# Sorting x by a permutation kept in fp32, in place of three bf16 parts of x

## The reference

```python
mask = (adj > 0.0).astype(x.dtype)
W1a, W1b = (W1[:F], W1[F:])
xj_proj = x @ W1a
diff = x[:, :, None, :] - x[:, None, :, :]
h = jax.nn.relu(xj_proj[:, :, None, :] + diff @ W1b + b1)
hm = jnp.einsum('bjkh,bjk->bjh', h, mask)
deg = jnp.sum(mask, axis=-1)
out = hm @ W2 + deg[..., None] * b2
x = _layernorm(x + out, axis=-1)
```

## Time and profile before

| | us |
|---|---|
| median of 3 runs (307.5 to 307.82) | 307.55 |
| the profiled execution | 308.28 |
| its span, first to last instruction | 306.2 |
| PE busy | 278.8 (91%) |
| DVE busy | 272.8 (89%) |
| ACT busy | 239.5 (78%) |
| POOL busy | 99.2 (32%) |

### The profile page before, as it was taken

The page is one execution under the profiler, slowest core; times in us unless marked ns, Lnnn a source line. Parts: engine busy times, 40 slices in busy tenths (PEclk is TensorE's granted clock), DMA queues, the critical chain, the costliest instruction groups (busy, mean ns, idle before and its releaser), DMA issues. The chain is left out here.

```text
span 306.2 us, 9122 instructions
## 1 busy us (share of the span) xinstructions
PE 278.8 (91%) x2601; PEld 209.3 (68%) x2601; DVE 272.8 (89%) x987; ACT 239.5 (78%) x706; POOL 99.2 (32%) x166
## 2 busy tenths in 40 slices
PE   0496999999999999999999999999999999999960
PEld 0253676877777877868787777777786877776750
DVE  2886699999999999999999999999999999989761
ACT  2338788889898989899898989898979889876500
POOL 1306142313334342434232343433342323304111
PEclk9999899999999999999999999999999999999985
DMA  7920303030211303030402112030304020100000
GB/s 205 371 99 1 89 0 105 3 98 9 57 66 28 96 19 106 14 108 0 120 0 79 40 35 85 17 103 17 103 1 120 0 56 2 35 3 18 19 17 21
DMA packets 28833, 18.12 MB, mean 59 GB/s; under 512 B 17537, under 2 KB 28033, under 8 KB 28802
## 3 DMA queue, kind: packets, MB, share of 16 engines
q1 hardware_dynamic: 28802, 17.76, 19.7%
HBM read 15.65 MB, written 2.10 MB: 58 GB/s over the span
## 5 line engine op out<-in xcount | busy, mean ns | idle before, releaser
L1024 PE MATMUL ring<-hot,vh 128*128 128x256 bf16 (+3 forms) x448 | 96.7, 268 | 1.0 <-ACT ring L740 1.0
L1024 PE MATMUL ring<-hot,vl 128*128 128x256 bf16 (+3 forms) x448 | 96.2, 267 | 0.0
L740 ACT COPY ring<-um 128x512 f32<-128x512 f32 (+2 forms) x144 | 65.9, 474 | 19.5 <-DVE small L1302 10.8
L1293 DVE SCALAR_TENSOR_TENSOR sm<-ring,sm 128x512 f32<-128x512 f32 (+2 forms) x144 | 73.0, 507 | 7.0 <-PE ring L1024 3.3
L1293 DVE SCALAR_TENSOR_TENSOR st<-ring,st 128x256 f32<-128x256 f32 (+2 forms) x144 | 48.0, 334 | 5.5 <-PE ring L1030 2.1
L1024 PEld LDWEIGHTS ring<-hot,vh 128*128 128x128 f16 x448 | 43.9, 98 | 11.9 <-issue 7.3
L1269 DVE TENSOR_SCALAR hot<-slotT 128x1024 bf16<-128x1024 f16 (+2 forms) x144 | 49.2, 373 | 0.0
L740 ACT COPY ring<-ut 128x512 f32<-128x512 f32 (+7 forms) x128 | 38.5, 338 | 13.0 <-DVE st L1293 11.0
L1024 PEld LDWEIGHTS ring<-hot,vl 128*128 128x128 f16 x448 | 44.1, 98 | 2.6
L1030 PE MATMUL ring<-hot,vh 128*64 128x512 bf16 (+3 forms) x256 | 44.7, 353 | 0.0
L533 POOL TENSOR_TENSOR vl<-vf,vh 128x384 f16<-128x384 f32 x32 | 28.6, 914 | 47.0 <-ACT vh L702 47.0
(11 more groups left out here) (106 smaller groups left out, 560.6 us busy)
## 6 DMA issues: line engine op xcount, KB each, us to landing
adj_sb<-adj SPq DMA_DIRECT2D x16, 512.0 KB, 4.1
x_sb<-x SPq DMA_DIRECT2D x16, 128.0 KB, 2.2
x_all<-x SPq DMA_DIRECT2D x4, 512.0 KB, 7.9
xT_sb<-xT SPq DMA_DIRECT2D x16, 128.0 KB, 3.8
out<-o_sb SPq DMA_DIRECT2D x16, 128.0 KB, 2.0
wts<-weights SPq DMA_DIRECT2D x1, 513.0 KB, 4.8
cst_general<-general SPq DMA_DIRECT2D x1, 256.0 KB, 6.3
cst_half<-half SPq DMA_DIRECT2D x1, 113.5 KB, 3.5
```

The lines of the kernel that those rows point to most:

```text
L740: eng.copy(view(segment, ring[unit % BANKS]), u).then_inc(seeded, 1)
L1024: last = eng.matmul(b[:, g * n:g * n + n], part[side][:, g * NT + k, 0:P], selection(g * NT + k), start=(s == 0 and not seeds), stop=(s == ...
L1293: eng.scalar_tensor_tensor(out=to, in0=v, scalar=0.0, in1=to, op0=ALU.max, op1=ALU.add).then_inc(added[tile], 1)
```

## The change

`perm` is made in fp32. The upper 16 bits of an fp32 one or zero are a bf16 one or zero, so the three readers that need bf16 read every second bf16 number (`perm16`). `sort_x` multiplies x by `perm` once, both in fp32. The four functions that split x, their tiles and their semaphores are gone. Since `sort_x` now reads `x_sb` itself, the load of x two pairs later waits for it too.

```diff
-        perm = both("perm", [P, TILES, P], BF16)
+        perm = both("perm", [P, TILES, P])
...
+        def perm16(side, c):
+
+            return perm[side][:, c, :].bitcast(BF16).rearrange("p (r two) -> p r two", two=2)[:, :, 1]
+
...
                 if not pair.general and pair.follows(2):
                     eng.wait_ge(xb_ready, pair.n - 1)
+                    eng.wait_ge(xs_ready, pair.n - 1)
                 eng.dma_start(x_sb[pair.side][:, :, :], x_v[pair.data]).then_inc(x_loaded[pair.side], 16)
...
-            def rest_x(pair):
...
-                eng.tensor_tensor(xr[:, :, :], x_sb[pair.side][:, :, :], xh[:, :, :],
-                                  ALU.subtract).then_inc(xr_ready, 1)
-
-            def low_x(pair):
...
-                eng.tensor_tensor(xl[:, :, :], xr[:, :, :], xm[:, :, :], ALU.subtract).then_inc(xl_ready, 1)
...
             def residual(pair):
                 eng.wait_ge(db_ready, pair.n + 1)
+                eng.wait_ge(x_loaded[pair.side], 16 * (pair.half + 1))
...
-                if has(2):
-                    low_x(second)
...
-                    rest_x(third)
                     neg_keys(third)
                     degree_bias(third)
...
-                eng.copy(xh[:, :, :], x_sb[pair.side][:, :, :]).then_inc(xh_ready, 1)
...
-                eng.copy(xm[:, :, :], xr[:, :, :]).then_inc(xm_ready, 1)
...
                 if has(2):
-                    high_x(second)
                     copy_degrees(second)
...
                 if has(2):
-                    middle_x(second)
                     ranks(second)
...
                           last = eng.matmul((bx1, bx2)[g][:, at:at + P], mask[pair.side][:, g * NT + t, k * P:k * P + P],
-                                          perm[pair.side][:, g * NT + t, :], start=True, stop=True)
+                                          perm16(pair.side, g * NT + t), start=True, stop=True)
...
             def sort_x(pair):
-                eng.wait_ge(xl_ready, pair.n + 1)
+                eng.wait_ge(x_loaded[pair.side], 16 * (pair.half + 1))
                 eng.wait_ge(perm_ready, pair.n + 1)
                 eng.wait_ge(maskT_copied, 2 * pair.n + 2)
-                parts = (xh, xm, xl)
                 for t in range(NT):
-                    for s, part in enumerate(parts):
-                        for g in range(2):
-                            last = eng.matmul(bx2[g * F:g * F + F, t * P:t * P + P], part[:, g * NT + t, :],
-                                              perm[pair.side][:, g * NT + t, :], start=(s == 0),
-                                              stop=(s == len(parts) - 1), skip_group_check=True)
+                    for g in range(2):
+                        last = eng.matmul(bx2[g * F:g * F + F, t * P:t * P + P], x_sb[pair.side][:, g * NT + t, :],
+                                          perm[pair.side][:, g * NT + t, :], start=True, stop=True,
+                                          skip_group_check=True)
                 last.then_inc(xs_ready, 1)
...
-                    last = eng.transpose(to[:, c * P:c * P + P], perm[pair.side][:, c, :], ident[:, :])
+                    last = eng.transpose(to[:, c * P:c * P + P], perm16(pair.side, c), ident[:, :])
```

More of the change, by code:

```diff
@@ L299, in build @@
         db = both("db", [P, TILES, F])
[L301 to L304, removed]
         xs = sb("xs", [P, N])
@@ L358, in build @@
         db_ready, xb_ready = sem("db_ready"), sem("xb_ready")
-        xh_ready, xr_ready = sem("xh_ready"), sem("xr_ready")
-        xm_ready, xl_ready = sem("xm_ready"), sem("xl_ready")
         xs_ready, xs_copied = sem("xs_ready"), sem("xs_copied")
@@ L586, in _ @@
             eng.wait_ge(consts_loaded["single"], 16)
-            rest_x(Pair(0, 0))
             neg_keys(Pair(0, 0))
             degree_bias(Pair(0, 0))
-            low_x(Pair(0, 0))
-            rest_x(Pair(0, 1))
             neg_keys(Pair(0, 1))
             degree_bias(Pair(0, 1))
-            low_x(Pair(0, 1))
             low_v(Pair(0, 0), 0)
@@ L598, in _ @@
             residual(Pair(0, 0))
-            rest_x(Pair(0, 2))
             neg_keys(Pair(0, 2))
@@ L608, in general @@
                 degree_bias(pair)
-                rest_x(pair)
-                low_x(pair)
                 low_v(pair, 0)
@@ L809, in _ @@
             eng.wait_ge(consts_loaded["single"], 16)
-            high_x(Pair(0, 0))
             copy_degrees(Pair(0, 0))
-            middle_x(Pair(0, 0))
             ranks(Pair(0, 0))
@@ L819, in _ @@
             look_over(Pair(0, 0))
-            high_x(Pair(0, 1))
             copy_degrees(Pair(0, 1))
@@ L823, in _ @@
             copy_u_tail(Pair(0, 0))
-            middle_x(Pair(0, 1))
             ranks(Pair(0, 1))
@@ L834, in general @@
                 copy_degrees(pair)
-                high_x(pair)
                 ranks(pair)
-                middle_x(pair)
                 for g in range(2):
@@ L914, in excesses @@
                     last = eng.matmul(bx3[:, c * P:c * P + P], deg16[pair.side][:, c:c + 1].to_broadcast([P, P]),
-                                      perm[pair.side][:, c, :], start=pair.general,
+                                      perm16(pair.side, c), start=pair.general,
                                       stop=(pair.general or c == TILES - 1), skip_group_check=True)
```

## The result

| | before | changed |
|---|---|---|
| median on the same chip, us | 307.69 | 310.43 |
| the profiled execution, us | 308.28 | 310.44 |
| its span, us | 306.2 | 308.4 |

The ratio is 1.0085 [1.0067, 1.0103]: slower by 0.9%, as forecast in sign; the time is 1.1 us above the 309.3 that I gave. A disturbed execution of the changed kernel (334.98 us) counts in the median of the table and not in the ratio; the other three have a median of 310.41.

What follows compares the result with a forecast made beforehand. PE was taken as the bound, with DVE close behind at 97%. Terms 1.7 + 0.3 + 0.1 - 0.3 gave +1.8 us: 310.1 for the profiled execution, 309.3 for the median, range 307.7 to 316.5.

Steps and rivals of the forecast that it cites:

- Sorting x: `sort_x` on PE: four fp32 matmuls take 0.59 us against 0.46, +0.13 us a pair, 1.7 us over thirteen bodies.
- side by side fails: Rival in `sort_x`: the fp32 column halves take turns, +0.56 us a pair, total 316.2 us; chance 0.12.
- Faster: Rival in `sort_x`: half-array fp32 passes take 0.055 us like bf16, -0.09 us a pair, total 306.0; chance 0.07.
- The start: Prologue: two sorts add 0.3 us, and the first `perm` ahead of the reductions adds 0.1 us.
- Reading `perm16`: PE's twelve matmuls a pair that stream `perm16` and four that load it: taken as zero extra cost.
- streaming with gaps: Rival on PE's twelve streaming matmuls: they go at fp32 pace, 0.64 us a pair, total 319 us; chance 0.08.
- slow loads: Rival on PE's four transposes: only their loads of `perm16` are slow, 0.25 us a pair, total 313; chance 0.08.
- DVE "hidden behind PE either way": DVE in each pair gains about 0.2 us at `hot` and loses 0.12 on fp32 `perm`, all hidden behind PE.
- The late waits: PE's 0.47 us of waits for DVE in the two long pairs: mostly taken up by DVE's new room, -0.3 us.
- ACT and POOL worth nothing: ACT loses `xh` and `xm`, POOL `xr` and its partner, in each pair; no effect on the time.
- The sum: Whole kernel: 1.7 + 0.3 + 0.1 - 0.3 = +1.8 us, forecast median 309.3 us.

Runs made afterwards that it cites:

- 1: Changed kernel with `perm` written in bf16 and widened by ACT to an fp32 copy for `sort_x` alone; steady pairs 16.815 us, total 311.81, ratio 1.0111.
- Experiment 5: Kernel before with DVE's `perm` ahead of `start_tail` from body 1 on, nothing else; pairs 16.683 us, total 307.9, ratio 0.9981.
- 2: Kernel before with `perm` in fp32 read through `perm16`, x still in three bf16 parts; pairs 16.740 us, total 310.0, ratio 1.0061.
- 3: Changed kernel with DVE's four `perm` instructions moved ahead of `start_tail`; steady pairs 16.833 us, total 311.9, ratio 1.0104.
- 4: Changed kernel with `perm` ahead of `start_tail` except in body 0, which keeps the old order; pairs 16.833 us, total 311.79, ratio 1.0107.
- 10: Kernel before with x in two fp16 parts and `perm` ahead of `start_tail` from body 1 on; twelve pairs 16.570 us apart, total 304.42, ratio 0.9882.

## Why the prediction came out as it did

**Sorting x: right.** Forecast +0.13 us a pair and 0.59 us in all, measured +0.131 and 0.590 in the change and in 1 alone. The reasons stood too: two passes, 0.85 ns a column, halves side by side, which came from fp32 on row halves and holds for column halves. The rival *side by side fails* is refuted in both orders of issue. *Faster* is refuted: a pass costs what its columns cost. In body 0 the wait for the bank covered it, as said: from the first matmul of `sort_x` to the gather is 0.932 us before and 0.933 after. In the prologue the two sorts cost 0.27 us more each, forecast 0.26. That PE is at the lower clock there I took from its steps, which are twice as long; the windows view gives 1.00 for that stretch.

**The start: the sum met by luck.** The prologue's terms came to 0.3 + 0.1, and the third head is 0.44 us later. But the 0.44 is made of other things as well, as the timeline of DVE shows, before:

```profile
7.98 0.58 DVE L1173 SCALAR_TENSOR_TENSOR w_abs<-wts 128x384 f32<-128x384 f32 x1 [1.98 <-DMA wts<-weights]
...
11.43 0.73 DVE L1167 TENSOR_SCALAR perm<-cst_half,rank 128x128 bf16<-128x128 f16 x4
```

and in the changed kernel:

```profile
9.43 0.56 DVE L1122 SCALAR_TENSOR_TENSOR w_abs<-wts 128x384 f32<-128x384 f32 x1 [3.62 <-DMA wts<-weights]
...
12.01 0.87 DVE L1116 TENSOR_SCALAR perm<-cst_half,rank 128x128 f32<-128x128 f16 x4
```

The weights land later, and the first `perm` starts 0.58 us later. Experiment 5, whose program is that of the kernel before up to there, has it at 12.22, so this is not the work of the change. From `perm` to the first head the changed kernel takes 0.33 us more (22.53 - 12.01 against 21.62 - 11.43); that much is near the forecast. From the first head to the second it takes 0.46 less, which is of the kind of the table above. The forecast's term was of about the right size, but the 0.44 does not show it.

**Reading `perm16`: mis-sized at zero, by a little.** The term should have been 12 x 0.0018 = 0.021 us a pair, 0.3 us over the kernel. Both rivals, *streaming with gaps* at 0.64 a pair and *slow loads* at 0.25, are refuted at this gap. My reason for zero was only half a reason: it left out that gaps do cost at some width, and at 8 bytes they would have cost 12 x 0.058 = 0.70 us a pair, more than the bound that I gave. The rule that I cited from the Trainium skill ("Advanced Engine Details and Errata", section "SBUF Cachelines") fits at 4 bytes, and does not fit at 8: two numbers still fall into each line of 16 bytes, and the matmul takes twice the time. The other rule, from "TensorE: Matmul & The Clock Gate" of the Trainium skill, section "Weight-path perf modes", I read too narrowly. The same table allows the columns of the weights to be "packed or strided", so it gave no ground for slow transposes; the trace agrees with the table, since they keep 0.056 us each with numbers 4 bytes apart.

**DVE "hidden behind PE either way": this step failed.** Its two sizes were right, `perm` at 282 ns and `hot` back at 0.39 us in all pairs. The second needed less than I thought: in 2, where `xr` still holds `db` back, `hot` takes 0.39 in all steady pairs too, since it now starts just ahead of `db`. The mistake was to add them. DVE meets PE twice in a pair, at `start_tail`, where it waits for `project`, and at `start_main`, for which PE waits. What DVE gains ahead of the first meeting turns into idle time there (0.36 us); what it loses between the two, the four `perm`, now 0.87 us and before 0.74, goes straight on. In the pair shown it had 0.14 us before, of which some 0.06 is the hand-over; now `start_main` ends 0.11 later, and PE's slower stream gives back only 0.014. The result is a wait of PE of 0.027 us in a steady pair, half of it ahead of the transposes and half among them, 0.3 us in all. It is shown by 3, where it goes when `perm` stands ahead of the meeting. I had written that the transposes are late next without cover, and had not seen that the cover lies on the wrong side.

**The late waits, forecast -0.3: failed, -0.07.** They were 0.30 + 0.16 and are 0.39 + 0. I took both for a lag of DVE that had built up over the pairs, which lighter work would take up. The second was DVE still behind from the first, held up once more where `hot` met `db` (236.53, in 2); it went with that meeting, in 2 as in the changed kernel. The first is a single late start of `start_tail`, at 6.26 us behind the head instead of 5.87, in both kernels alike; PE's `project` is on time there, and the profile puts the idle time of DVE to "issue", with no releaser. It has grown from 0.30 to 0.39 on PE because the fp32 `perm` leaves nothing to spare: 1, with `perm` in bf16, has 0.295, and 2, with fp32, has 0.393. Why it is late stays open. It is the `start_tail` of pair 12 (counted from 0), in the first body that DVE's list spells out behind its loop over pairs 4 to 11, and the late start is there in every kernel with `start_tail` ahead of `perm`; this points to the way out of the loop, but no run moves the end of the loop, so it is not shown. In 3, 4, 5 and 10, with `perm` ahead of it, it is gone. Whether that is because DVE has something to do then, or because the instruction stands elsewhere in the list, is not separated.

**ACT and POOL worth nothing: right.** Both are relieved and no distance on PE changes for it.

**The sum.** In the profile it is 1.7 (thirteen sorts, 0.131 each) + 0.4 (start) + 0.3 (stream) + 0.3 (wait) - 0.1 (late waits) - 0.4 (tail) = 2.2. My +1.8 had the first right and the second by luck; it lacked the next two, 0.6 together, took 0.2 too much for the late waits, and did not know of the tail. The medians differ by 2.7, since the profiled execution of before was 0.6 above its median and that of the changed kernel was not. Where start and tail move by more than that by themselves, this rest is not explained further.

## What to carry to other kernels

When an engine loses work at one place and gets some at another, do not sum over the loop: list the points at which it meets the engine that bounds the kernel, and sum between them. Gains ahead of a wait are lost in it; costs behind it are on the path, and moving the costly instruction to the other side of the wait can be worth more than making it cheap. Where two profiles differ by less than the start and the tail move by themselves, compare the distances from loop head to loop head.

## What the hardware did that I had not expected

- The price of a gap in PE's streamed operand: for 128 bf16 columns 0.0557, 0.0579, 0.1136 and 0.2254 us at 2, 4, 8 and 16 bytes from number to number. It doubles with each doubling from 4 bytes on. Loaded operands paid 0.005 to 0.01 us each at 8 and 16 bytes.
- The column halves of the array take fp32 matmuls side by side even when all matmuls of one half are issued first (0.597 against 0.590 us).
- A kernel whose thirteen pairs were 0.7 us shorter (3) had a median 1.5 us above the changed kernel's, with 1.5 us more in each of the start and the tail of its profile, where the low clock of PE lay at other instructions.
- DVE's `start_tail` begins 0.39 us late in one pair of sixteen, at the same place in the kernel before and after, with no releaser in the profile; it is DVE's first body behind its loop over pairs.
- In the steady pairs before and in 2, DVE's `hot` and POOL's `db` start within 0.08 us of each other. The one that starts first keeps its time (0.39 and 0.61 us), and the other is held up: `hot` then takes 0.81 to 0.86 us, `db` 0.79 to 0.86. A difference of 0.01 us in the start decides which.
